# Projections of the next stage inside the drain of both sixteen-head attentions

## The reference

```
x = x + tanh(g_xattn[l]) * attention_l(layernorm(x), ctx)
x = x + tanh(g_ffn[l])   * feed_forward_l(layernorm(x))
```

```
expert_out = silu(x @ expert_w[e].T + expert_b[e])
out = (sum over the best two of weight * expert_out) @ combine_w.T
```

## Time and profile before

| what | value |
|---|---|
| median of 3 runs | 1175.84 us (1175.04 to 1177.94) |
| the profiled execution: its time, its span | 1175.18 us, 1173.5 us |
| busy, share of the span: TensorE | 1088.6 us, 93% |
| VectorE, ScalarE, GpSimd | 62%, 60%, 40% |
| granted TensorE clock, mean | 0.975 |
| a2, f2, a3, f3 start at about | 690, 795, 865, 975 us |

### The profile page before, as it was taken

The page is one execution under the profiler, slowest core; times in us unless marked ns, Lnnn a source line. Parts: engine busy times, 40 slices in busy tenths (PEclk is TensorE's granted clock), DMA queues, the critical chain, the costliest instruction groups (busy, mean ns, idle before and its releaser), DMA issues. The chain is left out here.

```text
span 1173.5 us, 22877 instructions
## 1 busy us (share of the span) xinstructions
PE 1088.6 (93%) x8921; PEld 786.9 (67%) x8937; DVE 723.7 (62%) x1395; ACT 705.6 (60%) x1288; POOL 469.6 (40%) x741
## 2 busy tenths in 40 slices
PE   5998898899999999999997989988979988999998
PEld 2553478788888888888886646653646663466667
DVE  6774656566555665566663259974658994555554
ACT  4665621566666666666665568876448986644440
POOL 4872002223432223443344364431574534544440
PEclk7999999899999999999999999998989998999999
DMA  9200001000000000000000200000000000033320
GB/s 331 99 2 1 1 1 44 30 1 2 1 1 2 1 2 2 1 1 2 1 1 1 54 1 2 2 2 0 2 1 2 2 2 1 11 104 100 99 72 19
DMA packets 13885, 29.42 MB, mean 25 GB/s; under 512 B 2738, under 2 KB 5074, under 8 KB 13011
## 3 DMA queue, kind: packets, MB, share of 16 engines
q1 hardware_dynamic: 13778, 27.96, 7.1%
HBM read 25.14 MB, written 1.25 MB: 22 GB/s over the span
## 5 line engine op out<-in xcount | busy, mean ns | idle before, releaser
L1342 POOL TENSOR_TENSOR work<-work 128x1024 f32<-128x1024 f32 x64 | 121.3, 1896 | 268.2 <-DVE work L1436 268.2
L1423 DVE TENSOR_REDUCE work<-psum 128x8 f32<-128x1024 f32 x64 | 78.1, 1220 | 86.2 <-PE psum L1222 86.2
L1364 ACT ACTIVATE work<-work 128x1024 f32<-128x1024 f32 x64 | 67.4, 1053 | 95.8 <-DVE work L1427 95.8
L1434 DVE TENSOR_REDUCE work<-work 128x8 f32<-128x1024 f32 x64 | 77.4, 1210 | 71.7 <-ACT work L1364 71.7
L1807 PEld LDWEIGHTS psum<-w_down,work 128*128 128x128 f32 x768 | 99.1, 192 | 27.1 <-issue 25.6
L1807 PE MATMUL psum<-w_down,work 128*128 128x128 f32 x768 | 100.2, 275 | 1.1 <-DVE x L1932 0.7
L1119 DVE TENSOR_REDUCE work<-psum 128x8 f32<-128x1024 f32 x64 | 75.4, 1220 | 23.7 <-PE psum L874 23.5
L1067 ACT ACTIVATE work<-psum 128x512 f32<-128x512 f32 x128 | 74.3, 598 | 21.3 <-PE psum L888 20.9
L888 PEld LDWEIGHTS psum<-ident,work 128*128 128x128 f32 x512 | 57.2, 142 | 40.3 <-issue 21.5
L1427 DVE TENSOR_TENSOR work<-psum,work 128x1024 f32<-128x1024 f32 x64 | 78.4, 1225 | 6.7 <-DVE work L1423 0.5
L888 PE MATMUL psum<-ident,work 128*128 128x128 f32 x512 | 76.2, 280 | 5.4 <-ACT work L1067 3.6
(11 more groups left out here) (349 smaller groups left out, 2443.9 us busy)
## 6 DMA issues: line engine op xcount, KB each, us to landing
work<-chosen SPq DMA_DIRECT2D x80, 128.0 KB, 2.9
x<-in_x SPq DMA_DIRECT2D x2, 512.0 KB, 6.2
ctx_tok<-in_ctx SPq DMA_DIRECT2D x2, 512.0 KB, 8.2
xnt<-in_xt SPq DMA_DIRECT2D x1, 1024.0 KB, 10.1
ctxt<-in_ctxt SPq DMA_DIRECT2D x1, 1024.0 KB, 11.7
mask<-in_mask SPq DMA_DIRECT2D x1, 1024.0 KB, 10.0
w_down<-in_down SPq DMA_DIRECT2D x1, 1024.0 KB, 7.2
ctx_tok<-in_g SPq DMA_DIRECT2D x1, 1024.0 KB, 4.8
```

The lines of the kernel that those rows point to most:

```text
L1342: pool.tensor_tensor(prob[:, u % 2, h, :], prob[:, u % 2, h, :], rinv[:, u % 2, h].unsqueeze(2).broadcast_to([P, 8, P]), ALU.mult)\
L1423: dve.tensor_reduce(nmax[:, u % 2, h], s, AX.X, ALU.max, negate=True).then_inc(S["max"], 1)
L1434: dve.tensor_reduce(rsum[:, u % 2, h], prob[:, u % 2, h, :], AX.X, ALU.add).then_inc(S["sum"], 1)
```

## The change

For both a2 with f2 and a3 with f3:

- Three pieces of the next stage's projections (a piece is one projection of 512 tokens; in f3 a tile has two) stand inside the attention's part of TensorE's queue: in the last block, behind it, and ahead of the last turn back. The remaining pieces of `early` tiles (7 pieces in all for f2, 8 for f3) stand in the opening of the feed-forward, behind the logits of three groups and ahead of the tail of the attention. VectorE copies each raw into the ring, between the last residuals and behind them; the second projections of f3 go into `raw_second`, the room of weights that are no longer read.
- ScalarE's opening in f2 and f3 has no activations any more. In f2 the exponential of the routing stands directly behind the scores, then the activations of tiles 7 to 14, then the functions of the seven tiles that were put by. In f3 the functions of the four tiles stand directly behind the scores, ahead of the activations, and one sigmoid of a 128x1 probe stands in the opening.
- f2 has 15 tiles ahead instead of 12. f3 keeps 16.
- The eight steps of a3's mask move from the start of f2's part of VectorE's queue to m = 12 of its loop.
- GpSimd multiplies the first four tiles of f3 by the raw second projection.

f0 and f1 issue the same instructions as before. The diff, cut to its core:

```diff
 def small_head_attention(k, prev, tag, sub, names, bias_q, bias_k, bv, bo, mask_rows, set_mask, weights_of, selectors,
-                         turn_mask=None):
+                         next_stage, pieces, turn_mask=None):
...
@@ -948,6 +951,9 @@
                 turn(b - 1, 0)
                 if b >= 3:
                     turn_back(b - 3)
+                if b == NB:
+                    pe.wait_ge(S["sub"], 2 * NB)
+                    k.made[next_stage].early_up(pe, 0)
                 if at := fills(b):
                     if b >= 3:
                         pe.wait_ge(S["on"], b - 2)
@@ -969,10 +975,12 @@
                     pe.wait_ge(S["pt"], 4 * b - 1)
                     after.turn(pe, (b - 7) // 2)
                 gather(b - 1)
+        k.made[next_stage].early_up(pe, 1)
         turn_back(NB - 2)
         out(NB - 2)
         turn_to_tokens(NB - 1)
         after.turn(pe, NB // 2 - 3)
+        k.made[next_stage].early_up(pe, 2)
         turn_back(NB - 1)
         out(NB - 1)
         after.turn(pe, NB // 2 - 2)
@@ -1131,11 +1139,16 @@
                 residual_of(b - 3)
             if b >= 2:
                 normalise_of(b - 2)
+        k.made[next_stage].put_by(dve, 0)
         residual_of(NB - 3)
         normalise_of(NB - 2)
+        k.made[next_stage].put_by(dve, 1)
         residual_of(NB - 2)
         normalise_of(NB - 1)
+        k.made[next_stage].put_by(dve, 2)
         residual_of(NB - 1)
+        for piece in range(3, pieces):
+            k.made[next_stage].put_by(dve, piece)
         yield
...
+
+    def first_function(self, act):
+
+        act.activation(self.probe, self.k.floor[:, :], ACT.Sigmoid)
...
 def feed_forward(k, prev, tag, sub, tiles, function, ahead, lags, one_down=False, routing=None, spare=(), bias=None,
-                 requantise=None, joint=False, on_act=False, head=None, early=0):
+                 requantise=None, joint=False, on_act=False, head=None, early=0, given=0, raw_second=(), mask_at=0):
...
+    LATE = {1: 0, 3: 1, 5: 2, 7: 3}[sub]
...
+    PER = 2 if second else 1
...
-    head = head or B
+    head = head or early or B
...
     def wait_ready(eng, n):
 
-        if n < early:
+        if second:
+            eng.wait_ge(S["prod"], n + 1)
+        elif n < early:
             eng.wait_ge(S["early"], n + 1)
         else:
-            eng.wait_ge(S["prod"] if second else S["act"], n - early + 1)
+            eng.wait_ge(S["act"], n - early + 1)
...
     def up(pe, n):
+        for piece in range(PER * n, PER * n + PER):
+            project(pe, piece)
+
+    def project(pe, piece):
+        n, other = divmod(piece, PER)
         g, j = divmod(n, J)
         tokens = slice(g * GT, (g + 1) * GT)
-        if early and n == 0:
-            pe.wait_ge(k.late[0], k.late_count[0])
+        if early and piece == 0:
+            pe.wait_ge(k.late[LATE], k.late_count[LATE])
         if prev and j == 0:
             prev.ready(pe, g)
+        if other:
+            if 2 <= n < 2 + early:
+                pe.wait_ge(S["raw"], piece - 3)
+            elif n >= 2:
+                pe.wait_ge(S["second"], n - early - 1)
+            pe.matmul(bank[2 + n % 2][:, :], tiles[j][2], k.xnt[:, tokens], start=True, stop=True)\
+              .then_inc(S["up2"], 1)
+            return
         if B <= n < B + early:
-            pe.wait_ge(S["raw"], n - B + 1)
+            pe.wait_ge(S["raw"], PER * (n - B) + 1)
         elif n >= B:
             pe.wait_ge(S["act"], n - B - early + 1)
         pe.matmul(up_banks[n % B][:, :], tiles[j][0], k.xnt[:, tokens], start=True, stop=True)\
           .then_inc(S["up"], 1)
-        if second:
-            if n >= 2:
-                pe.wait_ge(S["second"], n - 1)
-            pe.matmul(bank[2 + n % 2][:, :], tiles[j][2], k.xnt[:, tokens], start=True, stop=True)\
-              .then_inc(S["up2"], 1)
-
-    def put_by(dve, n):
-
-        dve.wait_ge(S["up"], n + 1)
-        dve.tensor_copy(ring[n], up_banks[n % B][:, :]).then_inc(S["raw"], 1)
+
+    def put_by(dve, piece):
+
+        n, other = divmod(piece, PER)
+        if other:
+            dve.wait_ge(S["up2"], n + 1)
+            dve.tensor_copy(raw_second[n], bank[2 + n % 2][:, :]).then_inc(S["raw"], 1)
+        else:
+            dve.wait_ge(S["up"], n + 1)
+            dve.tensor_copy(ring[n], up_banks[n % B][:, :]).then_inc(S["raw"], 1)
...
         if routed:
-            pe.wait_ge(k.late[{1: 0, 5: 2, 7: 3}[sub]], k.late_count[{1: 0, 5: 2, 7: 3}[sub]])
-            if head == B:
+            pe.wait_ge(k.late[LATE], k.late_count[LATE])
+            if sub != 1:
                 r.logits(pe, prev, range(NG - 1))
+        for piece in range(given, PER * early):
+            project(pe, piece)
         for n in range(early, head):
             up(pe, n)
-        if routed and head > B:
+        if sub == 1:
             r.logits(pe, prev, range(NG - 1))
...
                 act.wait_ge(S["up2"], n + 1)
-                if n >= 2:
+                if n >= early + 2:
                     act.wait_ge(S["prod"], n - 1)
                 act.activation(u[:, n % 2, :], bank[2 + n % 2][:, :], ACT.Copy).then_inc(S["second"], 1)
...
+        def take_function(n):
+            j = n % J
+            act.wait_ge(S["raw"], PER * n + PER)
+            act.activation(ring[n], ring[n], function, bias=tiles[j][1] if tiles[j][1] is not None else 0.0)\
+               .then_inc(S["early"], 1)
+
         for n in range(early, head):
             activate(n)
-        yield
+        if second and early:
+            r.first_function(act)
+        yield
+        functions = iter(range(early))
         if routed:
             r.scores(act)
+            if early and one_down:
+                r.exponential(act)
+        if second:
+            for n in functions:
+                take_function(n)
         for n in range(head, ahead):
-            if n == 4 and one_down:
+            if n == 4 and one_down and not early:
                 r.exponential(act)
             activate(n)
-        for n in range(early):
-            j = n % J
-            act.wait_ge(S["raw"], n + 1)
-            act.activation(ring[n], ring[n], function, bias=tiles[j][1] if tiles[j][1] is not None else 0.0)\
-               .then_inc(S["early"], 1)
+        for of in functions:
+            take_function(of)
         if routed:
             r.keep(act, 0)
...
         yield
-        yield
         if routed:
             r.choose(dve)
         for m in range(N + LAG + TURN + 1):
+            if m == mask_at:
+                yield
...
         def multiply(n):
-            pool.wait_ge(S["second"], n + 1)
-            pool.tensor_tensor(ring[n % R], ring[n % R], u[:, n % 2, :], ALU.mult).then_inc(S["prod"], 1)
+            if n < early:
+                pool.wait_ge(S["early"], n + 1)
+            else:
+                pool.wait_ge(S["second"], n - early + 1)
+            pool.tensor_tensor(ring[n % R], ring[n % R], raw_second[n] if n < early else u[:, n % 2, :], ALU.mult)\
+                .then_inc(S["prod"], 1)
...
-    return Stage(tensor, scalar, vector, gpsimd, sync, ready, all_added, over, up, put_by)
+    return Stage(tensor, scalar, vector, gpsimd, sync, ready, all_added, over, project, put_by)
...
+                                        k.set_full_mask, 2, (8, 128), 2, 7, k.turn_full_mask)
...
         def f2(prev):
-            return feed_forward(k, prev, "f2", 5, up2, ACT.Silu, ahead=12, lags=(4, 7, 8), on_act=True, one_down=True,
-                                spare=(k.big[0], k.big[2], k.negb),
+            return feed_forward(k, prev, "f2", 5, up2, ACT.Silu, ahead=15, lags=(4, 7, 8), on_act=True, one_down=True,
+                                early=7, given=3, mask_at=12, spare=(k.big[0], k.big[2], k.negb),
...
+                                        k.set_key_mask, 3, (32, 64), 4, 8)
...
         def f3(prev):
-            return feed_forward(k, prev, "f3", 7, up3, ACT.Silu, ahead=16, lags=(0, 0, 0),
+            return feed_forward(k, prev, "f3", 7, up3, ACT.Silu, ahead=16, lags=(0, 0, 0), early=4, given=3,
+                                raw_second=[w[n][:, h * GT:(h + 1) * GT] for n in ("wq1", "wk1") for h in range(2)],
```

More of the change, by code:

```diff
@@ L81, in __init__ @@
         self.floor = sb("floor", [P, 1])
+        self.probe = sb("probe", [P, 1])
         self.mask2 = sb("mask2", [P, T], I32)
```

5 lines of the change are left out of this document (2 added, 3 removed).

## The result

The changed kernel takes 1184.06 us (median of 4 runs, 1183.53 to 1185.41); the kernel before took 1175.44 beside it (4 runs, 1172.43 to 1177.94). The ratio is 1.0073, 95% interval 1.0054 to 1.0092: slower by 8.6 us, with a bound of 0.3% for no change. The prediction was 1176.6, and 1184.06 lies above the end of its range, 1182.0. The profiled execution of the changed kernel took 1183.65, its span is 1181.9, 8.5 more than before; its mean granted clock is 0.974 (0.975 before).

The account below looks back on a forecast made before the run. TensorE, busy for 93% of the span, was taken as the bound. f2 at +3.0 and a3 with f3 at -2.2 summed to +0.8: 1176.0 us on the profiled execution, 1176.6 beside the median, range 1171.5 to 1182.0.

Parts of the forecast that it names:

- the last turns: Drains of a2 and a3: TensorE's last turn earlier by 2.45 and 2.4 us at full clock.
- The clock behind the pause: f2: TensorE idles about 4 us before the first selection, and the lower clock behind it costs +1.5 (0 to 2.0).
- The three projections fewer: f2: 16 projections done instead of 13 leave 2.6 us less to do, 0.4 of it lost again before the second add.
- The mask's stall: f2, m=12: the mask delays weighing 12, so TensorE stalls 2.1 us before tile 14's selection (0 to 3.1).
- The end of f2, put at nothing: Behind f2's second add: no term of its own; f2's sum of +3.0 was worked out for its middle.
- Exponential to first weights: f2, ScalarE: seven functions ahead of the first copy of combination weights lengthen this stretch by 4.4 us (3.8 to 4.6).
- the hold-ups of VectorE and GpSimd: f3's routing: GpSimd's multiplications end some 1.3 us before it, so its last steps run free: -0.5 (-2.0 to +1.5).
- a small rival: f3's routing: GpSimd's first four multiplications block VectorE's steps; +3.5 or so, 1180; chance 0.08.
- The clock behind f3's pause: f3: TensorE waits 3.5 us for the routing instead of 1.32, and the clock may fall: +0.7 (0 to 1.5).
- the slower rival: Drains of a2 and a3: the clock falls in both all the same; price 5.75, to 1182.3; chance 0.17.
- the faster one: f2's waits are absorbed: mask lands in slack, clock survives both pauses; 1172.3, or 1170.8 without f3's hold-ups; chance 0.20.
- the last one: Drains: they do not shorten at all, since VectorE's copies hold up residuals; 1180.6; chance 0.05.

Follow-up runs that it names:

- filler: Changed kernel plus four unused 128x512 multiplications in TensorE's pause in f2 and four in that of f3: 1179.26 us, ratio 1.0029.
- mask0: Changed kernel with a3's mask made right behind f2's routing, ahead of the first weighing, instead of at m = 12: 1179.85 us, ratio 1.0043.
- ahead12_mask0: Changed kernel with 12 tiles ahead in f2, not 15, and a3's mask ahead of the first weighing: 1179.14 us, ratio 1.0026.
- mask0_lags10: Changed kernel with a3's mask ahead of the first weighing and f2's layer norm turn ten steps behind, not eight: 1177.03 us, ratio 1.0023.
- keep_first: Changed kernel with f2's first copy of combination weights ahead of the seven functions: 1183.33 us, ratio 1.0072.
- hold5: Changed kernel with f3's GpSimd multiplications held from the sixth on until VectorE's four masking multiplications are done: 1183.01 us, ratio 1.0062.
- a_only: Only the change in a2 and f2; a3 and f3 as in the kernel before: 1182.47 us, ratio 1.0059 to the kernel before.
- hold4: Changed kernel with f3's GpSimd multiplications held from the fifth on until VectorE's four masking multiplications are done: 1180.97 us, ratio 1.0035.
- b_only: Only the change in a3 and f3; a2 and f2 as in the kernel before: 1175.11 us, ratio 1.0003 to the kernel before.

## Why the prediction was wrong

What the runs bear out: the granted clock of 1.00 in both drains; the last turns 2.3 and 2.2 us earlier (797.52 against 801.10 and 988.18 against 982.73, each less the shift of the attention's last block, -1.28 and +7.69; -2.45 and -2.4 predicted); the exponential 2.7 earlier (2.8); the seven functions' 4.38; the idle 4.15 with a clock of 0.57 behind it; the stall of 2.28 at tile 14. Three more terms of f2 came as forecast up to the second add. The clock behind the pause cost 1.48 in the changed kernel's trace (19.49 against 18.01 in filler), 1.5 predicted, and 1.3 to 2.8 over all traces. The three projections fewer gave 2.27 between the first two adds (9.90 in mask0, 12.17 before), 2.2 predicted. The mask's stall was 2.28, and 2.43 by the second add, 2.1 predicted. What failed, by the prediction's own steps, f2, +3.0 predicted and +9.0 measured:

- **The end of f2, put at nothing.** The steps on the projections and on the mask were worked out for the middle of f2 and carried to its end. Behind the second add the changed kernel loses 4.06 more: 3.25 without the mask (19.99 in mask0, 16.74 before) and 0.81 with it. The projections had covered TensorE's wait for root, scaling and turn of the layer norm, eight steps behind. But most of the price is again the clock: 2.54 of the 4.06 is the same work at the low level, behind waits of 2.15 and 3.08. 1.65 of it comes behind a wait that the kernel before has too, where its clock stayed up (ahead12_mask0). mask0_lags10 gives back 2.4 of the 3.25 by a later turn.
- **Exponential to first weights.** The step had put only ScalarE's queue there, +4.4. The clock fell a first time in that stretch, in the changed kernel's trace and in two others, behind TensorE's wait of 1.90 for ScalarE (1.39 before): 1.69 us more.

With 0.3 more for the mask up to the second add, less 0.1 that the other terms came out better, these make the 6.0 by which f2 is off. So three of the four falls of the clock in f2 had no term in the sum, though the prediction said that above all the clock would make its number wrong.

In a3 and f3, -2.2 predicted and +0.8 measured: **the hold-ups of VectorE and GpSimd** were put at -0.5 and are +1.4. The prediction named the mechanism as a small rival, with 0.08, and took for its own case that the early multiplications would be over before the routing's last steps. They were, 2.2 us before its end, but ahead of that VectorE's four short multiplications each waited for one of an unbroken row. **The clock behind f3's pause** was put at +0.7 and cost 1.7.

The rivals: the clock did not fall in the drains, so the slower rival's place was wrong though its sign was right; the faster one had the mask and the clock cost nothing, and both cost at least what the main case said; the last one, that the drains do not shorten, is refuted by the two last turns. The misses are 6.0 in f2 and 3.0 in f3; with the 1.28 by which this execution was ahead at the start, 1176.0 + 9.0 - 1.3 = 1183.7, the changed kernel's profiled time (1183.65).

What stays open is when the clock falls. Between exponential and weights it fell in the traces of the changed kernel, keep_first and hold5, and not in a_only, mask0, filler, hold4 and mask0_lags10, whose order of work is the same there (11.83 in these five, 13.52 in the changed kernel and hold5). The Trainium skill, "TensorE: Matmul & The Clock Gate", section "Part 1: The HAM clock gate (the "warmup" mystery)", says of the start of a kernel that the number of multiplications at the low clock is run-variable for one and the same kernel; the traces show the like in the middle of one, and no run here tells what decides it. Open too is whether the change or chance makes the clock fall behind the wait of 3 us near f2's end, where it stayed up in the kernel before. The sizes in the list are differences between single traces and share this uncertainty of 1 to 2 us.

## What to carry to other kernels

Before work is moved ahead to shorten a queue, ask of each piece what it covers where it stands now: here three projections fewer saved 2.3 us in the middle of the stage, and 3.25 was lost at its end. A block of work on an engine that others wait for in order cost about the same in the two places where it stood here; spread it, one piece a step, between the operations that others wait for. Carry each term to the end of the stage and not to its middle. And price every long wait of TensorE, old ones too, at its length plus a possible fall of the clock behind it: here it fell behind waits of 1.90 to 4.23 us, though not each time, for 1.3 to 2.8 us; multiplications without use in a pause, into a free bank, saved that here and delayed nothing in f2.

## What was not expected of the hardware

- A pause of 4.15 us on TensorE cost 1.3 to 2.8 us more behind it, by the trace, since the clock stayed low in the work that followed (0.56 and 0.59 in two stretches of 4 us in mask0).
- The same wait of 3.0 us, with the same work around it, left the clock at 1.00 in two traces (before, b_only) and cost 1.65 us in ahead12_mask0. Waits of 1.90 and 2.28 us, too, had a fall behind them in some traces and none in others.
- The same instructions ahead of the change ended up to 5.7 us apart from one execution to another (a2's last residual, behind the pieces, between 790.73 and 796.39). Medians of few runs and spans of single profiles can't show an effect of 2 us; stretches between two instructions of one trace agree to 0.02 us where the clock is the same.
- Four multiplications of 128x128 on VectorE, 0.23 us each when GpSimd is still, took 1.28 each beside an unbroken row on GpSimd, and 0.49 each (1.97 for four) beside a row with pauses of 0.4 us between.
